# Loading the tiles' expert numbers in the last mixture of a two-layer attention and mixture-of-experts kernel: registers loaded bare in place of loads with a check behind each

## The chip, the cores and the metric

The kernel runs on one core of a Trainium2 chip. The time is the device time of that core in microseconds (us), the median of several runs. The profile is of one execution of the same program; its span is the time from the first to the last instruction on the core.

## The reference, cut to what matters

2 x 1024 tokens of 256 features in float32 go through four blocks, each added to its input: attention to a context of 77 rows, a mixture of 8 experts of which each token takes 2 (with a shared one), a second attention, and a second mixture. The change lies in the last block alone:

```python
logits = x2 @ router_w
probs = jax.nn.softmax(logits, axis=-1)
top_p, top_e = jax.lax.top_k(probs, K)            # K = 2 of E = 8 experts
...
for e in range(E):
    m = (se == e)[:, None]
    h = h + jnp.where(m, jax.nn.gelu(xd @ w_in[e] + b_in[e]), 0.0)
for e in range(E):
    m = (se == e)[:, None]
    y = y + jnp.where(m, h @ w_out[e] + b_out[e], 0.0)
y = y * sp[:, None]
out = jnp.zeros((T, Dm), x.dtype).at[st].add(y)
```

Which expert a token goes to is known at run time only. With H = D = 256 all eight experts' weights fit into the core's memory.

## The kernel before, in words

The class `Last` computes the last mixture. It splits the 2048 tokens. The last 512 of them (`CT = 4` groups of 128) are computed *densely*: every expert on every token, times a weight that is zero where the expert was not chosen (the loop `for r in range(E + 1)` on each engine, L1264 on TensorE, L1407 on VectorE). The other 1536 (`RT = 12` groups) are *routed*: GpSimd scatters each token's row twice, once for each of its experts, into a table in DRAM that is sorted by expert (L1486), and the table is cut into `TILES = 19` tiles of one expert each, 12 with 256 rows and 7 with 128. Which expert a tile belongs to is worked out by VectorE in `slots` and stands as 19 whole numbers in one row of memory, `self.eid` (written at L1169, told by the semaphore `s_eid`).

Both the engines that read an expert's own data need its number as an address, so in a register: TensorE for the weights `w1h`, `w1l`, `w2h`, `w2l`, VectorE for the bias rows `b1a` and `b2a`. They load all 19 numbers in one go between the dense and the routed part:

```python
pe.wait_ge(s_x, CT * E)        # L1303: VectorE has added the last dense result
pe.wait_ge(self.s_eid, 1)
expert = [bass.ds(pe.value_load(self.eid[0:1, n:n + 1], min_val=0, max_val=E - 1), 1) for n in range(TILES)]   # L1305
```

and the same on VectorE at L1431. One `value_load` is three instructions of the engine's sequencer: TENSOR_LOAD (memory to register), FUSED_REGOPS (three register operations that compare the number with 0 and 7) and SEQ_ASSERT (the check itself). So there are 57 on each of the two engines. The same three stand at L1828, once for each tile, on SyncE, ScalarE and VectorE in the first mixture, which the change doesn't touch.

Behind the loads the routed part runs as a pipeline over the tiles, one after the other on every engine, tied by semaphores: SyncE loads a tile's rows `xin` (L1245), TensorE transposes them (L1314), ScalarE rounds the transpose (`xh`, L1377), VectorE takes the rest (`xl`, L1439), TensorE multiplies by w1 (three products for each, L143 to L145), VectorE adds the bias (L1446), ScalarE applies the GELU (L1388), TensorE transposes again (L1334), ScalarE and VectorE split again (L1383, L1452), TensorE multiplies by w2, VectorE adds the second bias (`yo`, L1460), ScalarE scales by the gate (L1393), GpSimd scatters the result (L1495). ScalarE, GpSimd and SyncE load no expert number here. SyncE has the rows of tiles 0 and 1 loaded ahead (it only waits for the scatters); after tile 1's it stores the 512 dense tokens to the output (L1248, behind the same wait `s_x` as TensorE's). At the end SyncE reads the scattered results back (L1255), VectorE adds them (L1467, L1469), and SyncE stores the rest.

Of the kernel before, what the change touches and what calls it, by code (L numbers as in the profile page):

```python
# [39 lines left out]
E, TOPK = 8, 2  # L40
# [52 lines left out]
def run(nc, *stages):  # L93

    with nc.Block() as block:
        @block.sync
        def _(sp):
            for s in stages:
                s.sync(sp)

        @block.tensor
        def _(pe):
            for s in stages:
                s.tensor(pe)

        @block.gpsimd
        def _(pool):
            for s in stages:
                s.gpsimd(pool)

        @block.vector
        def _(dve):
            for s in stages:
                s.vector(dve)

        @block.scalar
        def _(act):
            for s in stages:
                s.scalar(act)
# [822 lines left out]
class Last:  # L942
# [8 lines left out]
    TILES = PAIRS + SINGLES  # L951
# [161 lines left out]
    def slots(self, dve, ps_c):  # L1113
# [55 lines left out]
        v.tensor_copy(self.eid[:], tile_e[:, :, 0]).then_inc(self.s_eid, 1)  # L1169
        dve.wait_ge(self.s_eid, 1)  # L1170

    def run(self, out):


        nc, g, L, sem, T, CT, RT = self.nc, self.g, self.L, self.sem, self.T, self.CT, self.RT
        C, M1, TILES, PAIRS = CT * P, L.m1, self.TILES, self.PAIRS
# [23 lines left out]
        with ExitStack() as ctx:  # L1200
# [10 lines left out]
            both = t8("both")  # L1211
# [18 lines left out]
            with nc.Block() as block:  # L1230
# [32 lines left out]
                def _(pe):  # L1263
# [38 lines left out]

                    pe.wait_ge(s_x, CT * E)  # L1303
                    pe.wait_ge(self.s_eid, 1)
                    expert = [bass.ds(pe.value_load(self.eid[0:1, n:n + 1], min_val=0, max_val=E - 1), 1) for n in range(TILES)]  # L1305
                    weights = lambda a, e, cs: a[:, e, cs].rearrange("p o x -> p (o x)")
                    for i in range(-1, TILES + 2):
                        n = i + 1
# [7 lines left out]
                        n = i  # L1316
# [11 lines left out]
                        n = i - 1  # L1328
# [7 lines left out]
                        n = i - 2  # L1336
# [60 lines left out]
                def _(dve):  # L1397
# [30 lines left out]
                                v.scalar_tensor_tensor(out=g.X[:, t, :], in0=ps_o[:, 1 - q, a, :], scalar=wt[:, t, r - 1:r],  # L1428
                                                       in1=g.X[:, t, :], op0=ALU.mult, op1=ALU.add).then_inc(s_x, 1)

                    expert = [bass.ds(dve.value_load(self.eid[0:1, n:n + 1], min_val=0, max_val=E - 1), 1) for n in range(TILES)]  # L1431
                    for i in range(-1, TILES + 2):
                        n = i + 1
                        if n < TILES:
# [5 lines left out]
                        n = i  # L1440
# [7 lines left out]
                        n = i - 1  # L1448
# [4 lines left out]
                        n = i - 2  # L1453
# [48 lines left out]
class Route:  # L1502
# [160 lines left out]
    def number(self, dve, ps_c):  # L1663

        v, g, m, c = self.nc.vector, self.g, self.m, self.chain
        link = c.link
        dve.wait_ge(self.s_ed, 1)
        link(dve, v.tensor_scalar(self.sf[:], self.ed[:], 1.0, None, ALU.add))
        link(dve, v.reciprocal(self.gates[:, 0, :], self.sf[:, :, 0]))
        link(dve, v.tensor_tensor(self.gates[:, 1, :], self.gates[:, 0, :], self.ed[:, :, 0], ALU.mult))  # L1670
        link(dve, v.tensor_copy(m.xn[:, :, GATE], self.gates[:, 0, :]))

        dve.wait_ge(self.s_ct, 1)
        run = (self.pro2, self.eq, self.tmp)
        link(dve, v.memset(run[0][:, 0, :], 0.0))
        link(dve, v.tensor_copy(run[0][:, 1:NT, :], ps_c[:, 1, 0:NT - 1, :]))
        offs = c.prefix(dve, run, NT)
        link(dve, v.tensor_tensor(self.n_e[:, :, 0], offs[:, NT - 1, :], ps_c[:, 1, NT - 1, :], ALU.add))
        link(dve, v.tensor_tensor(self.slot[:], ps_c[:, 0], offs[:], ALU.add))

        link(dve, v.tensor_tensor(self.over, self.n_e[:].to_broadcast([P, E, TOK // P]), g.iota_thr[:], ALU.is_gt))
        v.tensor_reduce(self.pairs[:], self.over.rearrange("p e (k h) -> p e k h", h=2)[:, :, :, 1], AX.X, ALU.add)
        v.tensor_reduce(self.units[:], self.over, AX.X, ALU.add).then_inc(self.s_num, 1)
# [478 lines left out]
def build(nc, t, out):  # L2162
    with ExitStack() as ctx:
# [19 lines left out]
        with ExitStack() as own:  # L2183
            attention_operands(nc, own, g, L0)
            run(nc, *attend(own, L0, Prepare(nc, g, t["x"], sem), None, None, None))
# [17 lines left out]
        with ExitStack() as own:  # L2203
            attention_operands(nc, own, g, L1)
            before = Reload(nc, own, g, m, L1, sem)
            run(nc, mixture, *attend(own, L1, None, before, early, mixture))
# [83 lines left out]
```

## Time and profile before

| what | us |
| --- | --- |
| median of 3 runs | 923.65 |
| lowest and highest run | 921.39, 929.4 |
| the profiled execution: its own time | 923.64 |
| the profiled execution: its span | 921.8 |
| mean granted TensorE clock in it | 0.947 of full speed |

Names of engines in the profile: PE is TensorE's multiplication and PEld its weight load, DVE VectorE, ACT ScalarE, POOL GpSimd, SP SyncE; a q behind a name (PEldq, DVEq) is that engine's sequencer, whose instructions are not counted as busy time. Times of rows are in us from the span's start, durations in us or, in the view of one line, in ns. "issue" is time in which an engine waited for nothing that the profile shows. Granted clock 1.00 is 2.4 GHz, 0.50 is 1.2 GHz.

### The profile page before, as it was taken

What the parts mean: (1) busy time and instruction counts of PE and PEld (TensorE: products, weight loads), DVE (VectorE), ACT (ScalarE), POOL (GpSimd) and SP (SyncE); (2) the same over time, 40 slices, a digit from 0 to 9 for tenths busy, and PEclk for the clock granted to TensorE, in tenths of its full rate; (3) what the DMA queues carried; (4) which work ended last, traced back from release to release, by engine and by line L of the source; (5) the groups of instructions that cost most, each with busy time, mean ns of one, the idle gap of its engine ahead of it and who ended that gap; (6) DMA issues with size and microseconds to landing.
All of it is one profiled execution on the core that took longest, in us unless ns stands there. A gap on an engine that the chain in (4) does not pass through costs nothing. (4 is left out here: it accounts for less than half of the span.)

```text
span 921.8 us, 17578 instructions
## 1 busy us (share of the span) xinstructions
PE 803.1 (87%) x5949; PEld 744.2 (81%) x5949; DVE 660.1 (72%) x1332; ACT 478.3 (52%) x1006; POOL 249.8 (27%) x219
## 2 busy tenths in 40 slices
PE   8988999996979999999999999977999547939970
PEld 6876899995679999999999999946888426939960
DVE  3974999996784447878888879777778676726653
ACT  3643333332455566777777767543555343615650
POOL 8410333321014520122333323210222005502441
PEclk9989999999899999999999999999999887978995
DMA  8990000000304266677777669360000313313336
GB/s 300 298 294 7 1 1 1 0 1 8 141 13 133 92 194 247 229 228 228 228 228 228 218 217 300 79 194 1 1 1 0 130 55 120 122 57 100 120 99 222
DMA packets 61986, 118.28 MB, mean 128 GB/s; under 512 B 8610, under 2 KB 47620, under 8 KB 55140
## 3 DMA queue, kind: packets, MB, share of 16 engines
q1 hardware_dynamic: 49956, 98.80, 32.4%
q0 software_dynamic: 9792, 16.58, 7.2%
q10 hardware_dynamic: 2176, 2.10, 0.7%
q8 instruction: 36, 0.59, 0.3%
q14 instruction: 26, 0.21, 0.1%
HBM read 85.08 MB, written 32.37 MB: 127 GB/s over the span
## 5 line engine op out<-in xcount | busy, mean ns | idle before, releaser
L143 PE MATMUL e_ps_h<-e_xh,e_w1h 128*128 128x256 f32 (+1 forms) x496 | 142.4, 287 | 5.5 <-issue 5.5
L144 PE MATMUL e_ps_h<-e_xl,e_w1h 128*128 128x256 f32 (+1 forms) x496 | 139.9, 282 | 0.0
L145 PE MATMUL e_ps_h<-e_xh,e_w1l 128*128 128x256 f32 (+1 forms) x496 | 139.5, 281 | 0.0
L1868 POOL DMA_INDIRECT accumulated<-m_yo,m_token x39 | 69.8, 1789 | 203.4 <-ACT m_yo L2008 175.0
L143 PE MATMUL e_ps_o<-e_w2h,e_hh 128*128 128x256 f32 x440 | 122.4, 278 | 0.0
L144 PE MATMUL e_ps_o<-e_w2l,e_hh 128*128 128x256 f32 x440 | 121.9, 277 | 0.0
L145 PE MATMUL e_ps_o<-e_w2h,e_hl 128*128 128x256 f32 x440 | 121.9, 277 | 0.0
L1988 ACT ACTIVATE e_hf<-e_ps_h,e_b1s 128x256 f32<-128x256 f32 (+1 forms) x248 | 97.9, 446 | 43.8 <-PE e_ps_h L145 43.6
L853 POOL TENSOR_TENSOR at_pr<-at_pr,at_inv 128x1168 f32<-128x1168 f32 (+2 forms) x48 | 58.6, 1235 | 222.5 <-DVE at_inv L793 222.5
L143 PEld LDWEIGHTS e_ps_h<-e_xh,e_w1h 128*128 128x128 f32 x496 | 95.7, 193 | 5.7 <-issue 5.7
L144 PEld LDWEIGHTS e_ps_h<-e_xl,e_w1h 128*128 128x128 f32 x496 | 95.7, 193 | 0.0
L145 PEld LDWEIGHTS e_ps_h<-e_xh,e_w1l 128*128 128x128 f32 x496 | 95.6, 193 | 0.0
L2050 DVE TENSOR_TENSOR e_hl<-e_hf,e_hh 128x512 fp32r<-128x512 f32 (+1 forms) x124 | 71.7, 625 | 23.4 <-ACT e_hh L1994 21.5
L143 PEld LDWEIGHTS e_ps_o<-e_w2h,e_hh 128*128 128x128 f32 x440 | 82.8, 188 | 0.0
L145 PEld LDWEIGHTS e_ps_o<-e_w2h,e_hl 128*128 128x128 f32 x440 | 82.7, 188 | 0.0
L144 PEld LDWEIGHTS e_ps_o<-e_w2l,e_hh 128*128 128x128 f32 x440 | 82.7, 188 | 0.0
L143 PE MATMUL at_ps_o<-B_high,at_ph 128*128 128x256 f32 x240 | 69.7, 290 | 12.0 <-DVE at_pl L797 11.8
L1994 ACT CAST e_hh<-e_hf 128x512 fp32r<-128x512 f32 (+1 forms) x124 | 71.1, 573 | 3.9
L145 PE MATMUL at_ps_o<-B_high,at_pl 128*128 128x256 f32 x240 | 67.1, 280 | 0.0
L144 PE MATMUL at_ps_o<-B_low,at_ph 128*128 128x256 f32 x240 | 66.9, 279 | 0.0
L2061 DVE TENSOR_TENSOR m_yo<-e_ps_o,e_b2s 128x512 f32<-128x512 f32 (+1 forms) x31 | 19.5, 631 | 60.8 <-PE e_ps_o L145 38.8
L143 PE MATMUL at_ps_s<-A_high,at_xh 128*128 128x512 f32 (+1 forms) x160 | 56.5, 353 | 3.5 <-DVE at_xl L753 3.5
(413 smaller groups left out, 2224.7 us busy)
## 6 DMA issues: line engine op xcount, KB each, us to landing
e_w1s<-in_m_w SPq DMA_DIRECT2D x24, 1024.0 KB
e_w2s<-in_m_w SPq DMA_DIRECT2D x24, 1024.0 KB, 7.1
slots_in<-zero SPq DMA_DIRECT2D x20, 258.0 KB, 8.9
last_slots_in<-zero SPq DMA_DIRECT2D x16, 258.0 KB, 8.0
e_xin<-slots_in SPq DMA_DIRECT2D x16, 258.0 KB
d_xin<-last_slots_in SPq DMA_DIRECT2D x12, 258.0 KB
d_results<-last_results SPq DMA_DIRECT2D x8, 384.0 KB, 6.8
as_wk<-in_a_wk SPq DMA_DIRECT2D x2, 1024.0 KB, 9.4
```

Of the source, the lines that this page charges most:

```text
L143: nc.tensor.matmul(out, lh, rh, start=start, stop=False)
L144: nc.tensor.matmul(out, lh, rl, start=False, stop=False)
L145: return nc.tensor.matmul(out, ll, rh, start=False, stop=stop)
L853: last = nc.gpsimd.tensor_tensor(e[:, :, j0:j1], e[:, :, j0:j1], inv[:, :, i:i + 1].to_broadcast([P, H, j1 - j0]), ALU.mult)
L1868: nc.gpsimd.indirect_dma_start(out=g.acc[a], out_offset=bass.IndirectOffsetOnAxis(ap=token[:, n, a:a + 1], axis=0), in_=yo[:, q, a, :], in ...
L1988: last = nc.scalar.activation(hf[:, c, 0:n], ps_h[:, (q * MP + mp) % 4, i, 0:n], L.func, bias=b1s[:, e, c:c + 1])
L1994: nc.scalar.copy(hh[:, q, ms, 0:n], hf[:, ms, 0:n]).then_inc(s_hh, 1)
L2050: nc.vector.tensor_tensor(hl[:, q, ms, 0:w], hf[:, ms, 0:w], hh[:, q, ms, 0:w], ALU.subtract).then_inc(s_hl, 1)
L2061: nc.vector.tensor_tensor(yo[:, 1 - q, 0:rows], ps_o[:, 1 - q, 0:rows], b2s[:, e, :].to_broadcast([P, rows, D]), ALU.add).then_inc(s_ev, 1)
```

## The change

A new method makes the 19 register values, with the range given to the builder but with the check at run time left out, and both engines use it:

```diff
+    def experts_of(self, engine):
+        of = lambda n: self.nc.values_load(self.eid[0:1, n:n + 1], engines=(engine,), min_val=0, max_val=E - 1,
+                                           skip_runtime_bounds_check_because="the slots' program bounds it from both sides")
+        return [bass.ds(of(n), 1) for n in range(self.TILES)]
...
                     pe.wait_ge(s_x, CT * E)
                     pe.wait_ge(self.s_eid, 1)
-                    expert = [bass.ds(pe.value_load(self.eid[0:1, n:n + 1], min_val=0, max_val=E - 1), 1) for n in range(TILES)]
+                    expert = self.experts_of(mybir.EngineType.PE)
...
-                    expert = [bass.ds(dve.value_load(self.eid[0:1, n:n + 1], min_val=0, max_val=E - 1), 1) for n in range(TILES)]
+                    expert = self.experts_of(mybir.EngineType.DVE)
```

The loads stay where they were, in the same number and order. The waits ahead of them stay too.

## Rows read from the trace of the kernel before

**Rows 1.** The page: busy time, and the granted clock in 40 slices.
```profile
PE 803.1 (87%) x5949; PEld 744.2 (81%) x5949; DVE 660.1 (72%) x1332; ACT 478.3 (52%) x1006; POOL 249.8 (27%) x219
PEclk9989999999899999999999999999999887978995
```

**Rows 2.** Chain that ended last, 812 to 838: start us, us, what.
```profile
814.63 0.33 DVE X L1428
814.96 13.14 issue
828.11 1.12 PE d_ps_h L1314 x4
829.25 0.59 ACT d_xh L1377
829.87 0.17 DVE d_token L1438
```

**Rows 3.** Waits, 813 to 830: us in total, times, longest.
```profile
ACT d_xh L1377 <- PE d_ps_h L1314: 19.5, 1, 19.5
DVE d_token L1438 <- ACT d_xh L1377: 14.9, 1, 14.9
PE d_ps_h L1314 <- issue: 14.1, 1, 14.1
```

**Rows 4.** L1305 on TensorE: count: ns min/median/max, first and last start.
```profile
L1305 PEldq TENSOR_LOAD <-d_eid x19: 294/301/728, 815.0 to 827.5; - x19
L1305 PEldq FUSED_REGOPS  x19: 146/146/165, 815.5 to 827.8; - x19
L1305 PEldq SEQ_ASSERT  x19: 18/18/32, 815.8 to 828.0; - x19
```

**Rows 5.** L1305 again, in the stretches 814:815.8, 815.8:817.5, 818.3:828.1 and 826.4:828.1.
```profile
L1305 PEldq TENSOR_LOAD <-d_eid x1: 488/488/488, 815.0 to 815.0; - x1
...
L1305 PEldq TENSOR_LOAD <-d_eid x2: 512/620/728, 815.8 to 816.9; - x2
...
L1305 PEldq TENSOR_LOAD <-d_eid x15: 294/301/308, 818.4 to 827.5; - x15
...
L1305 PEldq TENSOR_LOAD <-d_eid x3: 301/301/305, 826.2 to 827.5; - x3
```

**Rows 6.** L1431 on VectorE, the whole span.
```profile
L1431 DVEq TENSOR_LOAD <-d_eid x19: 296/304/910, 814.1 to 825.8; - x19
L1431 DVEq SEQ_ASSERT  x19: 23/23/39, 814.7 to 826.3; - x19
```

**Rows 7.** L1828, the first mixture's loads on SyncE and ScalarE.
```profile
L1828 SPq TENSOR_LOAD <-m_tile_expert x46: 74/272/675, 274.2 to 571.8; - x46
L1828 ACTq TENSOR_LOAD <-m_tile_expert x23: 276/283/487, 350.0 to 584.8; - x23
```

**Rows 8.** Busy time by stretch: PE, PEld, DVE, ACT, POOL, clock, DMA share, GB/s.
```profile
814.00:817.00 3.00, 0.04 (x1) 0.00 (x0) 0.88 (x2) 0.00 (x0) 0.00 (x0) 1.00 0.37 125
817.00:818.00 1.00, 0.00 (x0) 0.00 (x0) 0.00 (x0) 0.00 (x0) 0.00 (x0) 0.62 0.46 151
818.00:828.00 10.00, 0.00 (x0) 0.00 (x0) 0.00 (x0) 0.00 (x0) 0.00 (x0) 0.50 0.00 0
828.00:834.00 6.00, 5.11 (x23) 4.72 (x24) 1.73 (x7) 1.17 (x2) 0.00 (x0) 0.50 0.29 78
835.00:838.00 3.00, 3.00 (x27) 2.85 (x26) 2.02 (x5) 2.09 (x5) 0.00 (x0) 1.00 0.09 16
```

**Rows 9.** Timeline of SyncE's queue, 809 to 832.
```profile
810.07 0.89 SPq L1245 DMA_DIRECT2D d_xin<-last_slots_in  x2
814.98 0.39 SPq L1248 DMA_DIRECT2D out<-X  x1
830.73 1.21 SPq L1245 DMA_DIRECT2D d_xin<-last_slots_in  x2
```

**Rows 10.** Timeline of VectorE, 843.8 to 853.
```profile
844.52 0.68 DVE L1460 TENSOR_TENSOR m_yo<-d_ps_o,d_b_rows 128x512 f32<-128x512 f32 x1
848.59 0.68 DVE L1460 TENSOR_TENSOR m_yo<-d_ps_o,d_b_rows 128x512 f32<-128x512 f32 x1
```

**Rows 11.** Chain that ended last, 895 to 921.8.
```profile
908.59 8.33 DMA d_results<-last_results
917.93 0.96 DVE X L1469
```

## Prediction

> **What bounds the kernel now.** I read the page first, then the chain, then the waits of the stretch that the change touches. By the page TensorE is the busiest engine, at 87% of the span [rows 1]. That average says nothing of the place of the change, for there TensorE does not multiply at all. The chain that ended last has one piece of 13.14 us called "issue", from 814.96, where VectorE finishes the last dense addition (L1428), to 828.11, where TensorE begins the first transpose of the routed part [rows 2]. The reader is to see in the waits that three engines stand still together and that one of them is the root: ScalarE waits 19.5 us for TensorE's transpose, VectorE 14.9 us for ScalarE, and TensorE 14.1 us for nothing but its own issue [rows 3]. The view of line 1305 says what it issues: 19 TENSOR_LOADs, 19 FUSED_REGOPS and 19 SEQ_ASSERTs between 815.0 and 828.0 [rows 4]. So in this stretch the kernel is bound by TensorE's sequencer, and each instruction taken out of that row shortens the path by its whole length, as long as nothing else is late.
>
> **How the 13.14 us are made up.** The loads are 16 of about 0.301 us and three slow ones of 0.488, 0.512 and 0.728 us [rows 4, 5]: 4.82 + 1.73 = 6.54. The comparisons are 19 x 0.146 = 2.77, the checks 19 x 0.018 = 0.34 [rows 4]. Together 9.65 us, which leaves 13.14 - 9.65 = 3.49 us for the pauses between the 57 instructions, 0.061 us for each. A second way to the same number: from the load that begins at 818.4 to the one at 827.5 lie 14 steps [rows 5], 9.1 / 14 = 0.65 us for one step of load, comparison and check, of which 0.301 + 0.146 + 0.018 = 0.465 are the instructions, and a third of the rest is 0.062 us.
>
> **What the change removes.** On TensorE 19 comparisons and 19 checks, with a pause for each: 2.77 + 0.34 + 38 x 0.061 = 2.77 + 0.34 + 2.32 = 5.43 us. What is left in the gap is 13.14 - 5.43 = 7.7 us: 19 loads and 19 pauses. This supposes that a load holds the sequencer for its 0.301 us also if the next instruction doesn't need its result. The trace can't show that, as behind each of its loads stands the comparison of that very number. So I bound it from both sides. Below: loads whose latencies overlap would cost as little as the shortest sequencer row with its pause, 0.018 + 0.061 = 0.08 us each [rows 4], 1.5 us in all, and the last one's own 0.3 us on top. Above: each as long as the slowest that TensorE shows, 0.728 + 0.061 = 0.79 us [rows 5], 15.0 us in all, more than now. I take 0.301 + 0.061 = 0.36 us: in 107 loads on four engines the medians are 0.301, 0.304, 0.272 and 0.283 us [rows 4, 6, 7], all of one kind, as a round trip to memory has it.
>
> The Trainium skill has a sentence on each end. Its page "Perfetto Trace Analysis" ("Per-instruction lifecycle: what the profiler-reported window actually captures") says that for an instruction of the sequencer alone the profile shows only its execution, and that the sequencer is ready for the next one only after that: the loads would stand in a row, with a hidden pause between them, as the rows have it for load and comparison. Its page "Runtime: NRT & Kernel Launch" ("Instruction fetch mechanics") gives some 200 ns for each register loaded, also where many are loaded together. As an estimate from that figure the gap would be 19 x (0.20 + 0.06) = 4.9 us and the profiled time about 915.4 us; the trace has 0.301 us for the same thing, which decides.
>
> **VectorE** sheds the same 38 instructions. It is worth nothing on the path. Its loads run from 814.1 to 826.3 [rows 6] while it has no work, and its first need is at 829.87 [rows 2], so it ends 3.5 us early now. After, TensorE restarts near 822.7, and VectorE is needed 829.87 - 828.11 = 1.76 us later, at 824.4. Its own 19 bare loads take 19 x (0.304 + 0.06) = 6.9 us, and 0.6 us more for the long one of 0.910 us: until 814.1 + 7.5 = 821.6. It stays ahead by 2.8 us. If it alone kept its comparisons and checks, it would end at 826.3 and be late by 1.9 us.
>
> **The slow loads.** The three long loads lie at 815.0 to 817.5, beside the store of the dense tokens (issued at 814.98 [rows 9]; the DMA engines are busy in 814:818 and idle in 818:828 [rows 8]), and VectorE's longest, 0.910 us, is in the same stretch [rows 6]. The store stays at its place, so this price stays; bare loads follow one another faster, so one or two more may fall into that stretch, up to 0.4 us each. I count nothing in the sum and widen the range by 0.8 us.
>
> **What stands behind the gap.** Does the rest move up by the full 5.4 us? The rows of tiles 0 and 1 were issued at 810.07, twelve and more us before they would be used even then [rows 9]. Tile 2's load is issued at 830.73, after VectorE has read tile 0, so it moves along. From there to the end everything is tied by semaphores to the tiles: one tile each 848.59 - 844.52 = 4.07 us in the warm stretch [rows 10], and then the read-back of 8.33 us and the last addition [rows 11]. No wait there is for something with a date of its own.
>
> **The clock.** TensorE's granted clock falls from 1.00 to 0.50 in the slice 817:818, 3 to 4 us after its last product, and stays at 0.50 until 834, 6 us after work began again [rows 8]; 1.2 and 2.4 GHz. The shortened gap, 8.6 us from that last product to about 822.7, is still long past the fall, so TensorE begins cold as before and I give the clock nothing. The cold stretch may last some us more or less, as the moment of the rise meets the new start elsewhere. In it an instruction of TensorE takes 5.11 / 23 = 0.22 us against 3.00 / 27 = 0.11 warm [rows 8], but a tile takes 4.07 us warm, in part for other engines' sake; 2 us more of cold cost at most half of that, 1 us. It goes into the range.
>
> **The sum.** Against the profiled execution's own 923.64 us (span 921.8 and 1.8 around it; the median of the runs is 923.65, the same): 923.64 - 5.43 = 918.2 us, 0.6% less. From about 1% (9.2 us) on a measurement of this kernel can tell a change from none, since its three runs lie between 921.39 and 929.4.
>
> **Rivals.**
> *Overlap.* The bare loads don't hold the sequencer, and the gap shrinks to 1.5 + 0.3 = 1.8 us. TensorE would begin near 816.9, before the clock falls in 817:818, and some of the cold 6 us might go: the 23 instructions there would save 23 x 0.11 = 2.5 us [rows 8]. Time 923.64 - 11.3 = 912.3 us, or 909.8 with the clock. For it: the shortest load row is 0.074 us on SyncE [rows 7]. Against: that is one of 46, and a load which only deposits its request would not show 0.301 us each time. Chance 0.11.
> *Crowding, the slower side.* The two engines read the same row of memory. Now each load is followed by 0.3 us of register work and they meet seldom; bare, both load without pause. If that stretches the loads on TensorE from 0.30 to over 13.14 / 19 - 0.06 = 0.63 us each, the gap is longer than now; at the 0.728 us of the slowest row it is 19 x 0.79 = 15.0 us, and the time 923.64 + 1.9 = 925.5 us. For it: the loads beside the store's traffic did stretch. Against: the last three on TensorE, from 826.2 on, when VectorE had finished, take 0.301 us as all did from 818.4 on, when it had not [rows 5, 6]. So meeting costs nothing that shows. Chance 0.04.
> *Nothing is removed.* The loads made through the other call keep their comparisons, the builder having the range still to hold. Time 923.6 us. For it: the range is still given. Against: the diff asks for no check. Chance 0.05.
>
> **How the numbers follow.** The forecast has 0.80, by itself 915.5 to 920.5 us (the clock's 1 us, the slow loads' 0.8 us, a load of 0.27 us as on SyncE saving 19 x 0.03 = 0.6 us more, and a run's scatter). Overlap 0.11, nothing removed 0.05, crowding 0.04. The range that leaves out most of the overlap and takes in the unchanged case, but of crowding only the milder part, is 912.0 to 923.7 us. Faster by over 1% (under 914.4) is the overlap and a little scatter, 0.13. Slower by over 1% (over 932.9) is reached by no case; I leave 0.02 to scatter. Within 1%: 0.85.
>
> **What would show it.** In the profile after: line of `experts_of` with 19 TENSOR_LOADs on TensorE and 19 on VectorE, no FUSED_REGOPS or SEQ_ASSERT between them; consecutive loads 0.36 us apart; the "issue" piece of the chain 7.7 us in place of 13.14; the first transpose at about 822.7; the clock at 0.50 there; the distance from the first transpose to the end 93.7 us as before (921.8 - 828.1). A gap near 2 us would show overlap, steps over 0.69 us crowding. The sum is wrong if the gap shrinks as said and the 93.7 us grow.

## The result, and the profile after

The kernel after takes 921.31 us (median of 20 runs, 914.16 to 929.03) against 926.25 us before (median of 20 runs, 920.89 to 931.25): ratio 0.995, 95% interval 0.9928 to 0.9973. Faster by 0.5%, clear of noise and within 1%, as forecast. Of 926.25 us that is 4.6 us (2.5 to 6.7); the prediction had 5.4. Runs in a slower state of the chip (here the one of 929.03 us) count in the medians and are left out of all ratios.

The profiled execution took 914.16 us with a span of 912.3, which is 9.5 us under the one before. It must not be read as the gain. The chain that ended last in the kernel after, 809 to 822 (start us, us, what), answers to [rows 2]:

```profile
810.24 0.22 DVE X L1433
810.46 7.97 issue
818.43 1.10 PE d_ps_h L1319 x4
...
819.55 0.59 ACT d_xh L1382
...
820.17 0.17 DVE d_token L1443
```

The issue piece is 7.97 us and was 13.14, 5.2 us less. But it begins at 810.46 and began at 814.96: 4.5 us of the 9.5 came ahead of the change, in code that is the same. From the last dense addition to the end of the span it is 912.3 - 810.46 = 101.8 us after and 921.8 - 814.96 = 106.8 us before, 5.0 us less. That distance is the yardstick in what follows, as it leaves out the scatter of the stages ahead; it scatters itself by about 1.5 us (e2 below). How large the scatter ahead of it is, one row of `L1169` shows, where the expert numbers are written; here it is in the kernels before, after and e6:

```profile
L1169 DVE CAST d_eid<-d_tile_e x1: 164/164/164, 764.4 to 764.4; 1x19 int32<-1x19 f32 x1
```
```profile
L1169 DVE CAST d_eid<-d_tile_e x1: 164/164/164, 758.4 to 758.4; 1x19 int32<-1x19 f32 x1
```
```profile
L1169 DVE CAST d_eid<-d_tile_e x1: 161/161/161, 772.7 to 772.7; 1x19 int32<-1x19 f32 x1
```

The same instruction behind the same work comes at 758.4 in one execution and at 772.7 in another, 14 us apart. A change of 5 us is seen in the trace of its place, and in a mean over many runs, but not in two profiled times.

The loads of the kernel after, whole and then in the stretch behind the long ones, 813.3 to 818.5 (count, ns min/median/max, first and last start), answer to [rows 4 to 6]:

```profile
L1173 DVEq TENSOR_LOAD <-d_eid x19: 300/308/779, 809.6 to 816.4; - x19
L1173 PEldq TENSOR_LOAD <-d_eid x19: 296/302/892, 810.5 to 818.1; - x19
...
L1173 PEldq TENSOR_LOAD <-d_eid x14: 296/302/310, 813.4 to 818.1; - x14
```

Comparisons and checks are gone. On TensorE 13 steps from 813.4 to 818.1 are 0.36 us each, 0.302 of load and 0.06 of pause. So a load holds the sequencer though nothing needs its number yet. By the lifecycle of a sequencer's instruction in the Trainium skill ("Perfetto Trace Analysis", "Per-instruction lifecycle: what the profiler-reported window actually captures") the next instruction is taken up only after the last one's execution; the trace agrees, by the same 0.36 us.

The stretches of the kernel after (us, PE, PEld, DVE, ACT, POOL, granted clock, DMA share, GB/s) answer to [rows 8]:

```profile
814.00:815.00 1.00, 0.00 (x0) 0.00 (x0) 0.00 (x0) 0.00 (x0) 0.00 (x0) 0.76 0.00 0
815.00:818.00 3.00, 0.00 (x0) 0.00 (x0) 0.00 (x0) 0.00 (x0) 0.00 (x0) 0.50 0.00 0
818.00:824.00 6.00, 4.79 (x21) 4.43 (x22) 1.66 (x6) 1.17 (x2) 0.00 (x0) 0.50 0.31 82
824.00:825.00 1.00, 1.00 (x8) 1.00 (x7) 0.69 (x1) 0.05 (x1) 0.00 (x0) 0.62 0.11 35
825.00:828.00 3.00, 3.00 (x28) 2.92 (x27) 1.91 (x5) 2.09 (x4) 0.00 (x0) 1.00 0.02 2
```

The clock falls within the gap again, in 814:815, some 5 us after TensorE's last product (which ended at 809.55; before it was 3 to 4 us), and comes back some 6 us after TensorE's restart at 818.43, as it did after 828.11. And the warm loop has its old step, 838.89 - 834.82 = 4.07 us on VectorE [rows 10]:

```profile
834.82 0.68 DVE L1465 TENSOR_TENSOR m_yo<-d_ps_o,d_b_rows 128x512 f32<-128x512 f32 x1
838.89 0.68 DVE L1465 TENSOR_TENSOR m_yo<-d_ps_o,d_b_rows 128x512 f32<-128x512 f32 x1
```

### The profile page after: what moved, and what is told of

It reads as the page before. It is cut to its first block and busy times, and to the rows that moved or that the text cites. A ratio compares the mean times of both kernels' runs of the same rounds, so it can differ in the third digit from the quotient of the medians.

```text
span 912.3 us, 17502 instructions
## 1 busy us (share of the span) xinstructions
PE 803.5 (88%) x5949; PEld 745.2 (82%) x5949; DVE 660.8 (72%) x1332; ACT 479.2 (53%) x1006; POOL 262.9 (29%) x219
## 5 line engine op out<-in xcount | busy, mean ns | idle before, releaser
L1873 POOL DMA_INDIRECT accumulated<-m_yo,m_token x39 | 82.4, 2112 | 189.4 <-ACT m_yo L2013 160.7
```

The source lines that it names most:

```text
L1873: nc.gpsimd.indirect_dma_start(out=g.acc[a], out_offset=bass.IndirectOffsetOnAxis(ap=token[:, n, a:a + 1], axis=0), in_=yo[:, q, a, :], in ...
```

## Experiments

All ratios are to the kernel before on the same chip. The edits are shown against the kernel after, cut to what matters. "To the end" is the distance from the last dense addition to the end of the span, 106.8 us before and 101.8 after.

**One engine alone.** e1 takes the bare loads on TensorE and leaves VectorE's line as it was; e2 the other way round.

```diff
-                    expert = self.experts_of(mybir.EngineType.DVE)
+                    expert = [bass.ds(dve.value_load(self.eid[0:1, n:n + 1], min_val=0, max_val=E - 1), 1) for n in range(TILES)]
```

> Bare loads on TensorE alone; VectorE keeps its comparisons and checks. Theory (both engines' sequencers work serially, the later one sets the start of the routed part): TensorE's 19 loads end 8.0 us after the last dense addition, but VectorE's 57 instructions begin 0.9 us before that addition ends and take 12.2 us, so they end 11.3 us behind it, where the kernel after has VectorE's first routed instruction at 9.7 us. So 1.6 us of the 5.2 us are lost: first transpose about 8.0 us behind the addition, VectorE's first routed instruction at about 11.4 us, gain 3.6 us, ratio 0.996. Rival (VectorE's share is worth nothing, TensorE alone counts): VectorE's first routed instruction at 9.7 us, gain 5.2 us, ratio 0.994.

> Bare loads on VectorE alone; TensorE keeps its comparisons and checks. Theory: the issue piece stays at 13.1 us within 0.3, VectorE merely waits longer for ScalarE (about 14.9 us as before), ratio 1.000. Rival (the two engines' loads get in each other's way, so that a lighter VectorE helps TensorE): TensorE's step of 0.64 us gets shorter by 0.02 us or more, the piece 12.7 us or less.

e1 measured 0.997 (0.9928 to 1.0012). Its waits, 815 to 829 (us in total, times, longest), and the end of its chain there:

```profile
DVE d_token L1443 <- ACT d_xh L1382: 11.4, 1, 11.4
PE d_ps_h L1319 <- issue: 8.9, 1, 8.9
...
PE d_ps_h L143 <- DVE d_xl L1444: 2.5, 1, 2.5
```
```profile
826.26 0.30 DVEq L1436
826.87 0.30 DVEq L1436
...
827.73 0.60 DVE d_xl L1444
828.47 0.58 PE d_ps_h L143
```

TensorE stands still for 8.9 us by this view, which counts from its own last product, and so it does after; but VectorE comes 11.4 us behind its last addition where the kernel after has 9.7 (820.17 - 810.46), and the chain runs through VectorE's own sequencer. TensorE waits for it 2.5 us, where after it waits 0.8. The wait list names ScalarE for VectorE's idle time, which was long done; the chain names the true cause. So VectorE's checks are worth 1.7 us at that point once TensorE's are gone, as the theory says; the ratio's interval holds both the theory's 0.996 and the rival's 0.994 and decides nothing. To the end it is 104.5 us, 2.7 more than after. Some 0.7 us of the missing 1.0 lie in the clock: it comes back in 833:834, 5 us behind the product at 828.47, and in the kernel after in 824:825, 3 us behind the same product at 821.15; from that product to VectorE's first `yo` it is 10.2 us in e1 and 9.5 after.

e2 measured 1.0014 (0.9979 to 1.0049). Its chain, 812 to 828:

```profile
813.26 13.12 issue
826.38 1.12 PE d_ps_h L1319 x4
```

13.12 us: VectorE's lighter row helps TensorE's nothing. VectorE's loads ended at 819.5 there, so for the last 6.9 us TensorE loaded alone, at the same step of 0.64 us. To the end it is 108.3 us, 1.5 more than before with the same gap: in e2's chain tile 2's rows are 4.13 us on the way. So differences of this distance under about 1.5 us say nothing by themselves.

**More loads.** e3 loaded all numbers twice on TensorE.

> TensorE loads all 19 numbers twice, bare, and uses the second set; VectorE as in the kernel after. Theory (serial loads of 0.30 us and a pause of 0.06): 19 more steps, 19 x 0.36 = 6.9 us more, issue piece 14.9 us where the kernel after has 8.0, ratio to before 1.002. Rival (loads are cheaper in a long row, for instance since most of the 8.0 us is a fixed price at its start or the slow loads beside the store): clearly under 6.9 us more, piece 12 us or less.

This one missed: its trace shows 19 loads on TensorE, not 38, as the builder leaves out loads whose result nothing uses. So e3 is the kernel after once more: 0.9961 (0.9922 to 1.0000), gap 8.0 us, 102.2 us to the end. e5 uses both sets:

```diff
+                    other = self.experts_of(mybir.EngineType.PE)
                     expert = self.experts_of(mybir.EngineType.PE)
...
-                            e = expert[n]
+                            e = other[n]
                             pe.wait_ge(r_xl, n + 1)
```

> In e3 the builder dropped the second set of loads, as nothing used it. Here both sets on TensorE are used, one for the first products' weights and one for the second products'. Theory (serial, 0.30 us and a pause of 0.06 for each): 38 loads, issue piece 8.0 + 6.9 = 14.9 us, first transpose 14.9 us behind the last dense addition, ratio to before about 1.002. Rival (a long row is cheaper for each load): 12 us or less.

Measured 1.000 (0.9962 to 1.0039). Its loads and the chain, 821 to 838:

```profile
L1173 PEldq TENSOR_LOAD <-d_eid x38: 295/302/882, 821.7 to 836.2; - x38
```
```profile
821.70 14.81 issue
836.51 1.10 PE d_ps_h L1320 x4
```

19 more loads, 14.81 - 7.97 = 6.84 us more, 0.36 us each: a plain sum. To the end 108.7 us, 6.9 more than after: everything behind the gap moves with it, in this direction too.

**The long loads.** e6 issues the store of the dense tokens later.

```diff
-                        if n == 1:
+                        if n == 6:
                             sp.wait_ge(s_x, CT * E)
```

> The kernel after, with the store of the 512 dense tokens issued behind the load of tile 6's rows and not of tile 1's. Theory (the store's traffic is what makes the second to fourth load slow): loads 2 to 19 all take 0.30 us, only the first stays at 0.49, gap 19 x 0.36 + 0.19 = 7.1 us in place of 8.0. Rival (the slow loads have another cause, such as their place in the row or the other engine's loads): three slow loads as before, gap 8.0 us. The time moves by 0.9 us at most, which the timing doesn't resolve.

```profile
L1173 DVEq TENSOR_LOAD <-d_eid x19: 299/309/328, 820.8 to 826.9; - x19
L1173 PEldq TENSOR_LOAD <-d_eid x19: 294/302/488, 821.6 to 828.4; - x19
```

The long loads are gone on both engines, but for TensorE's first; the gap is 7.1 us. So the store's traffic is what made single loads take up to 0.892 us; it costs 0.9 us of the gap. TensorE's first load, 0.488 us, has another cause, which no run isolates. Ratio 0.9886 (0.9818 to 0.9955), from four runs; that it lies lower than the 0.993 which 5.2 + 0.9 us would give is within its interval. To the end 100.8 us, 6.0 less than before.

**No loads, and one load.** e4 uses expert 0 for every tile, `expert = [slice(0, 1)] * TILES` on both engines, so the choice of the expert is left out. e7 makes one call for all 19 registers:

```diff
-        of = lambda n: self.nc.values_load(self.eid[0:1, n:n + 1], engines=(engine,), min_val=0, max_val=E - 1,
+        _, of = self.nc.values_load_multi_w_load_instructions(self.eid[0:1, 0:self.TILES], engines=(engine,), min_val=0, max_val=E - 1,
...
-        return [bass.ds(of(n), 1) for n in range(self.TILES)]
+        return [bass.ds(v, 1) for v in of]
```

> No loads at all on either engine: both use expert 0 for every tile, so the routed part multiplies by the wrong expert's weights; same work otherwise. This gives the ceiling of the whole idea. Theory: the gap on TensorE falls from 8.0 us to that of one semaphore (about 0.3 us) and TensorE's granted clock doesn't fall, since it falls only 3 to 4 us after the last product; the 23 instructions of the cold 6 us save up to 2.5 us. Together 12.8 us under before without the clock and up to 15.3 with it, ratio 0.986 to 0.983. Rival (something else comes late once the gap is gone, such as the rows of tiles 0 to 2 or the store of the dense tokens): gap over 1 us and a ratio of 0.990 or more.

> One TENSOR_LOAD on each engine that fills all 19 registers, in place of 19 loads. Theory (each register is a round trip to memory for itself, whatever the instruction): the instruction takes about 19 x 0.2 to 0.3 us, 4 to 6 us, only 18 pauses of 0.06 us = 1.1 us go; gap 5 to 7 us. Rival (one instruction fetches its 19 neighbouring words together, and the price was one round trip for each instruction): under 1.5 us, gap under 2 us, the granted clock stays up, ratio to before about 0.986 as with no loads.

e4 measured 0.9846 (0.9788 to 0.9904), about 14 us, with 92.1 us to the end, 14.7 less than before. The gap of 13.1 us is nearly all of it. Its stretches and chain:

```profile
816.00:819.60 3.60, 2.76 (x24) 2.55 (x22) 2.53 (x6) 0.00 (x0) 0.00 (x0) 1.00 0.00 0
819.60:822.00 2.40, 1.17 (x9) 0.94 (x9) 1.03 (x7) 1.07 (x2) 0.00 (x0) 1.00 0.58 195
822.00:826.00 4.00, 2.96 (x24) 2.76 (x25) 1.33 (x4) 1.22 (x2) 0.00 (x0) 1.00 0.53 146
```
```profile
819.73 0.67 PE d_ps_h L1319 x4
...
821.27 0.60 DVE d_xl L1444
821.89 2.71 DMA d_xin<-last_slots_in
```

TensorE stays at clock 1.00. What is late next is in the chain: tile 2's rows, issued when VectorE has read tile 0 and 2.71 us on the way; TensorE waits 1.0 us for them. What the warm start is worth is read from TensorE's first transpose to VectorE's first `yo`, the first start in these rows of the kernel before and of e4:

```profile
L1460 DVE TENSOR_TENSOR m_yo<-d_ps_o,d_b_rows x19: 409/678/692, 840.4 to 900.9; 128x512 f32<-128x512 f32 x12, 128x256 f32<-128x256 f32 x7
```
```profile
L1465 DVE TENSOR_TENSOR m_yo<-d_ps_o,d_b_rows x19: 415/680/691, 830.9 to 891.4; 128x512 f32<-128x512 f32 x12, 128x256 f32<-128x256 f32 x7
```

It is 12.3 us before (840.4 - 828.11) and, by the same rows, 12.3 after and in e5, and 11.2 us in e4 (830.9 - 819.73); in e8 to e11 below, which start warm as well, it is 11.3 to 11.4. So the warm start is worth about 1 us, not 2.5.

e7 measured 0.9895 (0.9838 to 0.9952), 97.8 us to the end. Its loads, and two of its stretches behind the gap:

```profile
L1173 DVEq TENSOR_LOAD <-d_eid x1: 1820/1820/1820, 822.8 to 822.8; - x1
L1173 PEldq TENSOR_LOAD <-d_eid x1: 2837/2837/2837, 823.7 to 823.7; - x1
```
```profile
827.00:828.00 1.00, 0.64 (x6) 0.40 (x4) 0.15 (x2) 0.76 (x2) 0.00 (x0) 0.85 0.00 0
828.00:834.00 6.00, 5.17 (x24) 5.11 (x25) 2.35 (x10) 1.41 (x3) 0.00 (x0) 0.50 0.30 88
```

Neither side of the expectation: 2.84 us on TensorE, beside the store, and 1.82 on VectorE, so 0.15 and 0.10 us for a register where a load of its own takes 0.36 with its pause. The gap is 2.92 us, 10.2 less than before, yet only 9.0 us are won to the end. TensorE begins at 826.57 at clock 1.00, but its clock falls in 827:828 all the same and stays at 0.50 for the next 6 us; to the first `yo` it is 12.6 us, as from a cold start. So in this execution a gap of 2.9 us is still too long to keep the clock. The Trainium skill ("Runtime: NRT & Kernel Launch", "Instruction fetch mechanics") has about 200 ns a register, also in bulk, with a view to the registers that the runtime itself loads; here, from the core's own memory, it is half to three quarters of that.

**Other places for the loads.** e8 spreads the 19 bare loads over the dense part; e9 does the same with `value_load`, so with comparison and check; e10 makes e7's single load in the dense part; e11 makes each bare load in the routed part, just ahead of the tile's first products and first bias. e8's edit on TensorE (VectorE's is alike, behind its additions of round r):

```diff
+                        if r >= 2:
+                            if r == 2:
+                                pe.wait_ge(self.s_eid, 1)
+                            expert += self.experts_of(mybir.EngineType.PE, range(3 * (r - 2), min(3 * (r - 1), TILES)))
...
                     pe.wait_ge(s_x, CT * E)
-                    pe.wait_ge(self.s_eid, 1)
-                    expert = self.experts_of(mybir.EngineType.PE)
```

In e9 `of` is `lambda n: eng.value_load(self.eid[0:1, n:n + 1], min_val=0, max_val=E - 1)`; in e11 the loops have `e = expert[n] = expert_of(n)`.

> The 19 bare loads spread over the dense part on both engines, three behind each expert's second products (from the third round on), one behind the last. Theory (a sequencer that stands in a load doesn't stop the array as long as work is queued ahead of it): gap falls from 8.0 to under 1 us, the dense part stays as long as it is (about 5.6 us a round), ratio to before near that without loads, 0.986. Rival (TensorE's queue runs dry, the dense part is TensorE-bound and each load comes on top of it): rounds of 5.6 + 1.1 = 6.7 us, the gap's 8 us paid in the dense part, ratio as in the kernel after, 0.995; only the clock's part is won.

> As e8, with the 19 loads spread over the dense part on both engines, but checked as in the kernel before: three steps of 0.64 us, 1.9 us, on TensorE's sequencer behind each expert's second products. Theory (what stands beside queued work costs nothing; the place of the loads and not their check was the price): gap under 0.3 us, dense part from the first to the last addition 40.0 us as in e8 within 0.5, from the last addition to the end about 93.6 us, ratio to before about 0.984. Rival (1.9 us is more than TensorE's queue holds, so the array runs dry): the dense part grows by up to 7 x 1.9 = 13 us less what stays hidden, ratio 0.990 or more.

> The single TENSOR_LOAD of 19 registers of e7, issued in the dense part (third round on TensorE, second on VectorE) instead of behind it. Theory: the instruction of 1.8 to 2.8 us is hidden beside queued work or costs its length once; gap under 0.3 us, dense part 40.0 to 42.8 us, ratio 0.984 to 0.987, not to be told from e8. Rival (a load in the dense part holds up more than its own length, since VectorE's loads delay what TensorE waits for): dense part over 43 us.

> Bare loads, each made in the routed part just ahead of the tile's first products on TensorE and ahead of its first bias on VectorE. Theory (sequencers run ahead of their arrays there too): the gap is under 0.3 us and a tile takes 4.07 us as before or at most 0.36 more where the sequencer is not ahead: 19 x 0 to 0.36 = 0 to 6.9 us; from the last addition to the end 93.6 to 100.5 us. I take the lower half, 95 us, ratio 0.986. Rival (each semaphore wait in the pipeline makes the sequencer arrive just in time, so each load comes on top on both engines, one behind the other): 0.7 us for each tile, 107 us to the end, no gain against before.

In the table "dense part" is the distance from the first to the last dense addition, with TensorE's mean granted clock in it.

| kernel | ratio | interval | gap, us | to the end, us | dense part, us | clock there |
| --- | --- | --- | --- | --- | --- | --- |
| before | | | 13.14 | 106.8 | 38.6 | 1.00 |
| e4 no loads | 0.9846 | 0.9788 to 0.9904 | 0.05 | 92.1 | 40.0 | 0.96 |
| e8 bare, spread | 0.9842 | 0.9782 to 0.9903 | 0.05 | 93.6 | 40.0 | 0.96 |
| e9 checked, spread | 0.9849 | 0.9801 to 0.9897 | 0.05 | 93.8 | 39.3 | 1.00 |
| e10 one load, early | 0.9858 | 0.9809 to 0.9907 | 0.04 | 92.9 | 40.1 | 0.96 |
| e11 bare, at each tile | 0.9849 | 0.9772 to 0.9926 | 0.05 | 93.2 | 40.1 | 0.96 |

All four win 13 to 14 us to the end, where the kernel after won 5.0, and none can be told from e4, which loads nothing. The rivals have fallen: e8's, e9's and e11's ratios of 0.995, 0.990 and 1 lie outside the intervals (e9's just so), and e10's dense part is not over 43 us. e9's line of loads and the piece of its chain at the former gap:

```profile
L1174 PEldq TENSOR_LOAD <-d_eid x19: 296/301/547, 785.2 to 816.8; - x19
L1174 PEldq FUSED_REGOPS  x19: 146/146/165, 785.8 to 817.1; - x19
L1174 PEldq SEQ_ASSERT  x19: 18/18/32, 786.0 to 817.3; - x19
```
```profile
819.52 0.35 DVE X L1437
819.87 0.04 issue
819.92 0.67 PE d_ps_h L1322 x4
```

The 57 instructions are all there with their old lengths, and the first transpose follows the last addition by 0.05 us. What they cost in the dense part instead must be read at the same clock: in some executions TensorE is still at clock 0.50 for the first 3 us of that part, and the part is then 1.5 us longer whatever the loads. The dense parts of e4 and e8, then of before and e9 (us, PE, PEld, DVE, ACT, POOL, granted clock, DMA share, GB/s):

```profile
779.70:819.68 39.98, 39.06 (x252) 35.79 (x251) 27.33 (x54) 20.40 (x33) 16.75 (x19) 0.96 0.37 117
775.60:815.61 40.01, 39.09 (x252) 35.86 (x251) 27.28 (x54) 20.45 (x33) 17.28 (x19) 0.96 0.37 116
```
```profile
776.40:814.96 38.56, 37.63 (x252) 34.49 (x251) 27.30 (x54) 20.42 (x33) 17.00 (x18) 1.00 0.39 121
780.60:819.87 39.27, 38.12 (x252) 34.58 (x250) 27.76 (x54) 20.31 (x33) 17.09 (x19) 1.00 0.38 119
```

Bare loads cost nothing there: e8 takes 40.0 us as e4 does. e9's checked loads cost some 0.7 to 0.9 us: it takes 39.3 us, where before has 38.6 and e6, also at clock 1.00, 38.4 (its forecast of 40.0 us came from e8 with its colder start). A part of it can be seen. The first three checked loads, two of them of 0.484 us, last from 785.2 to 787.5, and TensorE then stands still for 0.21 us:

```profile
L1174 PEldq TENSOR_LOAD <-d_eid x3: 305/484/484, 785.2 to 786.9; - x3
```
```profile
787.39 0.12 PE d_ps_o L145
787.50 0.21 issue
787.72 0.47 PE d_ps_h L143
```

At the end of the dense part e9's chain runs through VectorE's additions and VectorE's own checked loads (816.56 to 819.52), which points to the rest; no run isolates it.

TensorE's array works off what its sequencer has queued ahead while that stands in a load. The Trainium skill gives TensorE's queue a depth of 64 ("TensorE: Matmul & The Clock Gate", "Architectural detail: the array is 16x 32x32, not 1x 128x128"). No run here measures that depth; e9 shows that 2.3 us of register work, as long as some 19 products of 0.12 us, was 0.21 us more than the products queued ahead and their start could cover.

## Why the prediction was right

- *The place and the bound.* TensorE's sequencer sets the stretch: e2 leaves its row and gains nothing, e5 lengthens it and loses what it adds.
- *The size.* Forecast 5.43 us off a gap of 13.14, measured 5.17 in the gap, 5.0 to the end, 4.6 (2.5 to 6.7) by the ratio. The missing 0.26 us is the step that was kept out of the sum and in the range: bare loads come faster, so those beside the store hit it harder. TensorE's 19 loads sum to 6.81 us and summed to 6.54; e6 shows that the store's traffic is the cause of slow loads. One reading was off without effect on the sum: the prediction puts all three slow loads beside the store, but the first, 0.488 us, stays when the store is moved.
- *A load holds the sequencer.* This was the one thing the trace of before could not show. The steps are 0.36 us, as taken. Overlap has fallen; so has crowding, since the medians are 302 ns with both engines loading without pause, and e2's row is no shorter when VectorE stops.
- *VectorE.* Worth nothing as long as it stays ahead, and late by 1.9 us if it alone kept its checks: e1 has 1.7, and 2.7 to the end.
- *What moves along.* Forecast 93.7 us from the first transpose to the end, measured 912.3 - 818.43 = 93.9. That they agree within 0.2 us is partly luck: with the same cold start e2 has 95.2 and e3 94.2.
- *The clock.* Nothing gained, as said: fallen before the restart, cold for about 6 us in both. With a gap of 2.9 us the clock is still lost (e7). The overlap rival's 2.5 us for a warm start was too much: e4 and e8 to e11, which stay warm, show about 1 us. That tile 2's rows take the rest is likely from e4's chain and not tested.
- *The median.* The forecast of 918.2 us was anchored at a median of 3 runs of before, 923.65; over 20 runs that is 926.25. The 3.1 us between forecast and measurement are mostly this. For the same reason 921.31 us lies inside the stated range but above the 915.5 to 920.5 us that the prediction gave its own forecast; and as the range took in the case that nothing is removed, the time alone bears out little. The trace of the gap does.

## What to carry to other kernels

Where the chain of waits says "issue" on a stretch in which every engine stands still, look at the sequencer's rows of that line: register loads, comparisons and checks add up one by one, and each has a pause of about 0.06 us that no row shows. Trimming such a row wins its trimmed part (here 5 us of 13), but moving it beside queued work wins nearly all of it and a warm start with it, and then the checks can stay: e9 keeps every check, wins 13.0 us to the end and pays 0.7 to 0.9 us ahead, some 12 us in all, more than twice what the change did. Judge an edit of a few us by the distance between two marks around it in the trace, not by two profiled times whose other stages scatter by more; and compare a stretch at the same granted clock, or the clock's share passes for the edit's.

## What the runs showed of the hardware

A load of one register from the core's memory takes 0.30 us on TensorE and VectorE and a pause of 0.06; one instruction that loads 19 neighbouring registers takes 1.8 to 2.0 us on VectorE and 2.3 to 2.8 on TensorE (e7, e10), so for each register a load of many is 2.4 to 3.6 times cheaper, the pause included. Traffic of the DMA engines (351 GB/s in the microsecond 816:817 of before) stretches single loads to 0.5 to 0.9 us. TensorE's sequencer can stand in register work, bare loads of 1.1 us at a time, in a part where the array is 98% busy, and the part gets no longer (e8); with checked loads of 1.9 to 2.3 us at a time it gets 0.7 to 0.9 us longer and the array runs dry once, for 0.21 us (e9). And TensorE, starting again at clock 1.00 after a gap of 2.9 us, lost the clock about a microsecond later (e7).
